# Conditional projection and LoRA, 64 samples on one core: order of SyncE, ScalarE and VectorE in the first two pairs, and two transfers for the adapter stack

## What is computed

```python
# x (64,128,1024) f32; itok_B_1_198, itok_B_0_6 (64,): one index per sample
x = x + einsum('bct,bcd->bdt', x, weights[itok_B_1_198])          # per-sample 128x128 matrix
H = einsum('btd,od->bto', x, W)                                   # W (1024,1024), dense
xa = einsum('btd,brd->btr', x, A[itok_B_0_6])                     # LoRA, rank 16, 8 adapters
x = x + H + einsum('btr,bor->bto', xa, Bm[itok_B_0_6]) * scalings[itok_B_0_6]
```

## Time and profile before

| what | before |
|---|---|
| median of 3 runs | 807.09 us |
| the profiled execution, its own time / its span | 807.68 us / 805.0 us |
| PE busy | 770.3 us (96%) |
| DVE / ACT / POOL busy | 620.4 / 510.4 / 190.7 us (77% / 63% / 24%) |
| chain that ended last | PE 89%, DVE 4%, SPq 3%, DMA 2% |
| first 100 us: PE / DVE / ACT busy | 70.6 / 72.1 / 45.2 us |

### The profile page before, as it was taken

The page is one execution under the profiler, slowest core; times in us unless marked ns, Lnnn a source line. Parts: engine busy times, 40 slices in busy tenths (PEclk is TensorE's granted clock), DMA queues, the critical chain, the costliest instruction groups (busy, mean ns, idle before and its releaser), DMA issues.

```text
span 805.0 us, 16851 instructions
## 1 busy us (share of the span) xinstructions
PE 770.3 (96%) x4456; PEld 728.9 (91%) x4456; DVE 620.4 (77%) x1397; ACT 510.4 (63%) x1186; POOL 190.7 (24%) x428
## 2 busy tenths in 40 slices
PE   6875799999999999999999999999999999999997
PEld 3565699999999999999999999999999999999996
DVE  5695977787877778788777878877787887777864
ACT  3364566667666666776666667666666766666663
POOL 4440211222222122222211222221122222112200
PEclk9888899999999999999999999999999999999998
DMA  8522134344233443432334343233434323343221
GB/s 289 149 93 85 59 119 138 117 143 142 97 106 117 137 133 128 143 105 98 123 129 143 117 143 116 99 124 120 140 117 143 134 93 118 117 137 117 86 87 78
DMA packets 47380, 98.26 MB, mean 122 GB/s; under 512 B 6788, under 2 KB 26244, under 8 KB 47364
## 3 DMA queue, kind: packets, MB, share of 16 engines
q1 hardware_dynamic: 47362, 98.08, 37.0%
q10 hardware_dynamic: 2, 0.00, 0.0%
HBM read 63.45 MB, written 34.60 MB: 122 GB/s over the span
## 4 chain that ended last, share of the span: by engine, by line
PE 89%; DVE 4%; SPq 3%; DMA 2%; issue 1%; ACT 1%; DVEq 0%; ACTq 0%
PE bank L1259 73%; PE o_ps L1295 4%; PE o_ps L1296 4%; PE o_ps L1297 4%; PE bank L1274 3%; SPq L343 1%; DVE x_lo L826 1%; DVE w_lo_raw L1089 1%; DMA out<-o_sb 1%; DMA cond_sb<-cond_idx 1%; DVE w_lo L826 1%; SPq L387 0%; PE bank L1279 0%; SPq L390 0%; ACT x_hi L475 0%
## 5 line engine op out<-in xcount | busy, mean ns | idle before, releaser
L1259 PE MATMUL bank<-w_hi,x_hi 128*128 128x342 f32 (+1 forms) x1240 | 404.5, 326 | 7.7 <-ACT c_sb L475 5.6
L1259 PE MATMUL bank<-w_lo,x_hi 128*128 128x342 f32 (+1 forms) x1240 | 401.4, 324 | 0.0
L1259 PE MATMUL bank<-w_hi,x_lo 128*128 128x342 f32 (+1 forms) x1240 | 400.9, 323 | 0.0
L1259 PEld LDWEIGHTS bank<-w_hi,x_hi 128*128 128x128 f32 x1240 | 234.7, 189 | 17.0 <-ACT c_sb L475 6.9
L1259 PEld LDWEIGHTS bank<-w_lo,x_hi 128*128 128x128 f32 x1240 | 234.4, 189 | 3.3
L1259 PEld LDWEIGHTS bank<-w_hi,x_lo 128*128 128x128 f32 x1240 | 234.7, 189 | 0.0
L826 DVE TENSOR_TENSOR x_lo<-x_raw,x_hi 128x256 fp32r<-128x256 f32 (+1 forms) x279 | 151.0, 550 | 34.2 <-ACT x_hi L475 28.9
L475 ACT ACTIVATE x_hi<-x_raw 128x256 fp32r<-128x256 f32 (+1 forms) x279 | 138.2, 507 | 55.7 <-PE bank L1259 49.8
L292 POOL TENSOR_TENSOR w_lo<-a_ride,w_hi 128x160 fp32r<-128x160 f32 x31 | 16.1, 521 | 541.6 <-ACT w_hi L475 541.6
L475 ACT ACTIVATE c_sb<-bank 128x342 f32<-128x342 f32 x190 | 85.5, 451 | 42.0 <-PE bank L1259 41.3
L475 ACT ACTIVATE o_sb<-o_ps 128x512 f32<-128x512 f32 x124 | 74.2, 598 | 36.2 <-PE o_ps L1297 27.0
(11 more groups left out here) (85 smaller groups left out, 846.5 us busy)
## 6 DMA issues: line engine op xcount, KB each, us to landing
x_raw<-xT SPq DMA_DIRECT2D x64, 512.0 KB, 4.6
out<-o_sb SPq DMA_DIRECT2D x62, 512.0 KB, 2.7
b_stack_raw<-b_split SPq DMA_DIRECT2D x128, 128.0 KB, 2.5
a_now<-lora_a SPq DMA_DIRECT2D x64, 64.0 KB, 3.2
c_raw<-cond_w SPq DMA_DIRECT2D x64, 64.0 KB, 1.8
w_lo_raw<-wB SPq DMA_DIRECT2D x7, 342.0 KB, 6.9
w_hi_raw<-wB SPq DMA_DIRECT2D x5, 342.0 KB, 6.7
out<-x_raw SPq DMA_DIRECT2D x4, 256.0 KB, 2.0
```

The lines of the kernel that those rows point to most:

```text
L1259: last = nc.tensor.matmul(bank[:, lo:hi], x[:, left, c * C:(c + 1) * C], w[:, c, FIRST[o]:FIRST[o] + WIDTH[o]], start=opens and c == 0 and ...
```

## The change

On SP:

- The first transfer is the block b12, then both samples of x. Block b01 and the table of scalings are issued by ACT. Block b21 is issued ahead of the first A, b11 ahead of `lora_b`.
- `b_split` is laid out with the part outermost, so that each part is one transfer of 512 KB. Both are issued ahead of pair 1's A and pair 0's condition matrices, which stood ahead of the sixteen before.
- In pair 1's step both stores of pair 0 stand ahead of pair 3's x, which is issued behind the second.

On PE only the dense blocks change places: b21 ahead of b30, and b31 and b02 ahead of the two `turn` products; b32 ahead of the first `lora`. On ACT, `take_b(0, 0)` moves behind the operands of pair 1, the rides and c, `in_place("9")` behind `copy_c17` to `whole_block("02")`, and `evacuate(0, 1, -1, 0, 1)` ahead of the hi parts of "19", "6" and "12". On DVE some sums and rests change places: "y" comes some twenty instructions earlier, `in_place("18")` and `rest_a001` later or earlier by a few instructions. On POOL the identity is added to b21 before the rides of the first pair. No computation is added or left out.

```diff
-    DENSE = ("b12", "b01", "b30", "b21", "b20", "b10", "b00", "b11", "b31", "b02", "b32", "b22")
+    DENSE = ("b12", "b01", "b21", "b30", "b20", "b10", "b00", "b11", "b31", "b02", "b32", "b22")
...
-        b_split = nc.dram_tensor("b_split", [NAD, 2, R, T], f32, kind="Internal").ap()
+        b_split = nc.dram_tensor("b_split", [2, NAD, R, T], f32, kind="Internal").ap()
...
 # SyncE
+            load_w(sp, "b12")
             load_x(0, 0, 0, 0)
-            load_w("b12")
             load_x(0, 0, 0, 1)
-            load_w("b01")
-            load_w("b30")
-            sp.dma_start(s_tab[:, :], scalings.to_broadcast([P, NAD])).then_inc(s_landed, 16)
+            load_w(sp, "b30")
+            load_w(sp, "b21")
             sp.wait_ge(adapter_landed, 16)
             load_a(0, 0, 0)
...
+            sp.wait_ge(b_hi_ready, 1)
+            sp.dma_start(b_split[0, :, :, :].rearrange("a r o -> (a r) o"), z_hi[0][:, :].bitcast(f32)).then_inc(b_saved, 16)
+            sp.wait_ge(b_lo_ready, 1)
+            sp.dma_start(b_split[1, :, :, :].rearrange("a r o -> (a r) o"), z_lo[0][:, :].bitcast(f32)).then_inc(b_saved, 16)
             sp.wait_ge(first_scaled, 8)
             load_a(0, 0, 1)
             sp.wait_ge(cond_landed, 16)
             load_c(0, 0, 0)
-            sp.wait_ge(b_hi_ready, 1)
-            for a in range(NAD):
-                sp.dma_start(b_split[a, 0, :, :], z_hi[0][a * R:(a + 1) * R, :].bitcast(f32)).then_inc(b_saved, 16)
-            sp.wait_ge(b_lo_ready, 1)
-            for a in range(NAD):
-                sp.dma_start(b_split[a, 1, :, :], z_lo[0][a * R:(a + 1) * R, :].bitcast(f32)).then_inc(b_saved, 16)
-            sp.wait_ge(b_saved, 32 * NAD)
+            sp.wait_ge(b_saved, 32)
             load_b(0, 0, 0)
             step(0, 0)
-            step(0, 1)
+            load_b(0, 1, 0)
+            store(0, 1, -1, 1)
+            load_a(0, 1, 2)
+            store(0, 1, -1, 0)
+            after(sp, lo_ready["u54"], 0, 1, 0)
+            after(sp, lo_ready["a02"], 0, 1, 0)
+            after(sp, lo_ready["u3"], 0, 1, 0)
+            load_x(0, 1, 2, 0)
+            load_x(0, 1, 2, 1)
+            load_c(0, 1, 1)
...
 # ScalarE
             act.dma_start(adapter_sb[:, :], adapter_idx).then_inc(adapter_landed, 16)
+            load_w(act, "b01")
+            act.dma_start(s_tab[:, :], scalings.to_broadcast([P, NAD])).then_inc(s_landed, 16)
...
             in_place("3")
-            hi_a1(0, 1, 1)
-            begin_c02(0, 1)
             evacuate(0, 1, -1, 0, 0)
             turned_xa(0, 1, 0, 1)
+            evacuate(0, 1, -1, 0, 1)
             made(act, "19", "12")
...
             in_place("12")
             hi_u12(0, 1, 1)
-            evacuate(0, 1, -1, 0, 1)
...
 # VectorE
             add("4", slot("lo", "4"), w_block("b11"), w_block("b12"), ALU.subtract)
-            in_place("2")
             made(dve, "i32")
             add("14", slot("lo", "14"), slot("hi", "12"), w_block("b32"), ALU.add)
-            in_place("0")
             in_place("4")
-            dve.wait_ge(w_landed["b31"], 16)
-            add("18", slot("lo", "18"), slot("hi", "12"), w_block("b31"), ALU.add)
+            dve.wait_ge(w_landed["b02"], 16)
+            add("y", slot("lo", "8"), w_block("b12"), w_block("b02"), ALU.subtract)
             in_place("14")
```

More of the change, by code:

```diff
@@ L363, in step @@
                     load_c(i, j, 1)
+            load_w(sp, "b12")
             load_x(0, 0, 0, 0)
-            load_w("b12")
             load_x(0, 0, 0, 1)
-            load_w("b01")
-            load_w("b30")
-            sp.dma_start(s_tab[:, :], scalings.to_broadcast([P, NAD])).then_inc(s_landed, 16)
+            load_w(sp, "b30")
+            load_w(sp, "b21")
             sp.wait_ge(adapter_landed, 16)
             load_a(0, 0, 0)
-            load_w("b21")
-            load_w("b20")
+            load_w(sp, "b20")
+            load_w(sp, "b11")
             sp.dma_start(b_raw[:, :], lora_b.rearrange("a r o -> (a r) o")).then_inc(b_raw_landed, 16)
-            for b in ARRIVAL[5:]:
-                load_w(b)
+            for b in ARRIVAL[6:]:
+                load_w(sp, b)
             sp.dma_start(cond_sb[:, :], cond_idx).then_inc(cond_landed, 16)
@@ L446, in _ @@
             pick_scalings(0, 0, 0)
+            pool.wait_ge(w_landed["b21"], 16)
+            add_identity("b21", 0, 170, 0, 128)
+            add_identity("b21", 1, 298, 0, 44)
             pool.wait_ge(a_landed, 32)
@@ L449, in _ @@
             first_rides("b30")
-            pool.wait_ge(w_landed["b21"], 16)
-            add_identity("b21", 0, 170, 0, 128)
-            add_identity("b21", 1, 298, 0, 44)
             first_rides("b20")
@@ L455, in _ @@
             first_rides("b00")
+            pool.wait_ge(w_landed["b11"], 16)
+            add_identity("b11", 0, 0, 86, 42)
+            add_identity("b11", 1, 42, 0, 128)
             pool.wait_ge(w_landed["b10"], 16)
@@ L711, in _ @@
             hi_of("13", slot("hi", "19"))
+            made(act, "5")
+            in_place("5")
             made(act, "v")
             in_place("15")
-            made(act, "5")
-            in_place("5")
             act.wait_ge(b_raw_landed, 16)
@@ L756, in _ @@
             hi_z12(0, 0, 0)
-            made(act, "9", "f")
-            in_place("9")
             copy_c17(0, 1)
@@ L1145, in _ @@
             first_rest(0)
+            add_identity_c(0, 0)
             sum_u910(0, 0, 1)
-            add_identity_c(0, 0)
             rest_u(0, 0, 1)
             sum_u11(0, 0, 1)
+            rest_c(0, 0)
             rest_u910(0, 0, 1)
-            rest_c(0, 0)
             rest_u11(0, 0, 1)
-            dve.wait_ge(w_landed["b02"], 16)
-            add("y", slot("lo", "8"), w_block("b12"), w_block("b02"), ALU.subtract)
-            in_place("18")
             made(dve, "y")
             add("10", slot("lo", "10"), slot("hi", "6"), slot("lo", "8"), ALU.subtract)
+            in_place("18")
             rest_u67(0, 0, 1)
@@ L1165, in _ @@
             add("11", slot("lo", "11"), slot("lo", "11"), slot("hi", "6"), ALU.add)
+            in_place("7")
+            rest_a001(0, 0, 1)
+            dense_through(dve, "b12", "b31")
+            add("12a", w_block("b31"), w_block("b31"), w_block("b32"), ALU.subtract)
+            rest_z("11", 0, 0, 0)
             rest_z("10", 0, 0, 0)
-            rest_z("11", 0, 0, 0)
-            rest_a001(0, 0, 1)
-            in_place("7")
-            dense_through(dve, "b12", "b31")
+            made(dve, "11a")
             add("9", w_block("b12"), w_block("b12"), w_block("b32"), ALU.subtract)
-            add("12a", w_block("b31"), w_block("b31"), w_block("b32"), ALU.subtract)
+            rest_a03(0, 0, 1)
+            rest_z("12", 0, 0, 0)
             in_place("11")
-            rest_z("12", 0, 0, 0)
-            rest_a03(0, 0, 1)
+            sum_u54(0, 0, 1)
             rest_z("01", 0, 0, 0)
             rest_z("00", 0, 0, 0)
-            sum_u54(0, 0, 1)
             made(dve, "12a")
@@ L1222, in _ @@
             rest_xa0(0, 1)
+            sum_u67(0, 1, 1)
+            rest_u12(0, 1, 1)
             sum_u910(0, 1, 1)
@@ L1402, in _ @@
             dense("b01")
+            made(pe, "i21b")
+            dense("b21")
             pe.wait_ge(first_scaled, 2)
             dense("b30")
-            made(pe, "i21b")
-            dense("b21")
-            pe.wait_ge(first_scaled, 8)
+            pe.wait_ge(first_scaled, 4)
             dense("b20")
+            pe.wait_ge(first_scaled, 6)
             made(pe, "i10")
             dense("b10")
+            pe.wait_ge(first_scaled, 8)
             made(pe, "i00")
@@ L1414, in _ @@
             dense("b11")
+            dense("b31")
+            dense("b02")
             pe.wait_ge(ident_r_ready, 1)
@@ L1417, in _ @@
             turn0(0, 0)
-            dense("b31")
-            dense("b02")
+            made(pe, "i32")
+            dense("b32")
             after(pe, g_ready[1], 0, 0, 0)
@@ L1424, in _ @@
             lora("12", 0, 0, 0)
-            made(pe, "i32")
-            dense("b32")
             made(pe, "i22")
```

77 lines of the change are left out of this document (40 added, 37 removed).

## The result

| what | before | after |
|---|---|---|
| median, same chip (four runs each) | 806.48 us (804.62 to 807.21) | 1013.88 us (1012.5 to 1015.24) |
| ratio, 95% interval | 1 | 1.2569 (1.2546 to 1.2593) |
| profiled execution, its span | 807.68 us, 805.0 us | 1014.96 us, 1012.9 us |

The forecast was 791.0 us, with a range of 786.5 to 798.0. The prediction was wrong by 223 us, in the sign and in the place: the first two pairs did become shorter, and the loop, which it had set aside, lost 7.4 us a pair (from one copy of the adapter stack to the next 30.73 us for 23.35, mean of 24 pairs).

The account below looks back on a forecast made before the run. PE was taken to bound the loop, left alone, and DVE's queue the first pairs, where only waits could go. Gains 8.1 + 6.0 + 1.3 + 1.3 = 16.7 us from 807.7 gave 791.0 us, range 786.5 to 798.0.

Parts of the forecast that it names:

- Stores ahead of pair 3's x: Pair 1's step: earlier store ends ACT's 9.25 us wait for `o_sb` and DVE's wait before "19"; gain 8.1 us (7.0 to 8.1).
- Adapter stack in two transfers and later copy: First pairs: sooner stores and later `take_b` cut DVE's 6.92 us wait to some 0.9; gain 6.0 us (4 to 6.9).
- First transfers and sums: DVE's first stretch: reordered transfers and sums remove part of 2.5 us of waits; gain 1.3 us (0 to 2.5).
- b01 on a second queue: First transfers: b01 on ACT's queue gains nothing; by the skill page's rule the sum would be 1.1 us smaller.
- DVE's waits on PE: Pair 1: DVE's 1.12 us wait before `xa_sum` and some tenths beside it go; gain 1.3 us (0 to 1.3).
- saturated stretch: PE's nearly gapless run from 98.45 us to the end, busy 701 of 707 us; forecast to begin near 82 us.
- PE becomes the bound: Rival, pair 1: DVE lighter than counted, PE's own 24.0 us set the end; 788 us or less, chance 0.08.
- The clock never comes up in pair 1: Slower rival: granted clock 0.50 throughout pair 1, its 24.0 us of PE work becoming 48; 812 us, chance 0.04.

Follow-up runs that it names:

- four blocks: The kernel before with the adapter stack in four blocks of 8 rows a read and 32 small stores: 826.86 us, ratio 1.0239.
- eight-read kernel: The changed kernel with each read of 32 rows made as two reads of 16 rows, layout kept: 788.44 us against 807.76, ratio 0.9765.
- the kernel with x first: The eight-read kernel with SP again issuing pair 3's x ahead of sample 1's store in pair 1's step: 799.22 us, ratio 0.990.
- The kernel with the old layout: The changed kernel with the adapter outermost in DRAM, one-piece reads of 32 rows, and two stores of 8 blocks each: 790.75 us, ratio 0.9783.

## Why the prediction was wrong, point by point

**The step that failed** is in two sentences. "[...] the change leaves the loop alone, so nothing can be won there": `load_b` is called for every pair, and the diff changed its layout. And the price of "the stack's reads, which took 4 us from the first issue at 33.70 to the copy at 37.72": these rows are of a read of 32 rows in one piece, and were used for a read that goes over two pieces. The new layout was costed as a change of the stores alone. As measured the term is 12.9 us for 4.0 us, and it applies to all pairs, not to pair 0 alone. The numbers to see that the loop was at risk stood in the trace: in the loop of before ACT comes to the copy 6.13 us or 6.75 us behind the issue, so a read that takes 4 us is hidden, and one of 12.9 can't be. Put in full on each pair, the difference would be some 6.8 us (12.9 - 6.13), against 7.4 measured. The rival that was missing is "slower, by the stack's read in the loop": as an estimate, 791.0 + 31 x 6.8 = 1002 us, against 1013.9 measured. That this comes out so near is partly luck: in the loop the read takes 14.1 us from issue to copy and not 12.9, and with four blocks the same subtraction would give 2.75 us a pair where 0.47 was measured. The eight-read kernel against after is 225 us, for the form of one access.

All the prediction's rivals lie in pairs 0 to 2. The prediction drew on the page "DMA: Bandwidth & Descriptors" of the Trainium skill, from another section than the one that states the rule, and did not hold the new access against the rule.

**The rest of the prediction** can be held against the eight-read kernel, which does all that the change does but for that read (and issues eight reads where the change has four): 788.4 us (789.0 in the later runs) for a forecast of 791.0.

- *Stores ahead of pair 3's x, 8.1 us (7.0 to 8.1).* Right as to the mechanism, and too small: 8.7 us alone, 10.8 us when undone in the full version, both above the upper end. The term was sized by the wait in the trace of before; once the first wait is gone the second would have been longer, so the two terms don't simply add.
- *Adapter stack in two transfers and later copy, 6.0 us (4 to 6.9).* Right as to the mechanism: the stack is no longer waited for, and both halves of the edit are needed (3.9 and 4.0 us, each undone by itself). No run undoes both. What stands on record is the kernel with x first, which has all but the stores: 7.9 us less than before (807.10 - 799.22), where this term, the next one and that of the waits on PE come to 8.6 us together. (It takes DVE's first block as ended at 33.67; the row gives 33.76, 33.34 + 0.42, which changes nothing.) What the prediction said would stay did not: A was to land at 27.4 and the rides to be ready at 33.3, "of the 6.92 us some 0.9 stay". In the eight-read kernel (POOL's first and last step of the rides):

```profile
25.84 1.86 POOL L268 TENSOR_TENSOR a_ride<-a_now,s_now 128x32 f32<-128x32 f32 x3 [0.44 <-DMA a_now<-lora_a]
...
30.33 0.58 POOL L288 TENSOR_TENSOR a_ride<-a_now,a_ride 128x32 f32<-128x32 f32 x1
```

  A is there at 25.84 and the rides at 30.9, not 33.3, and DVE has no wait between 23.59 and 71.97. SP issues A at 21.53 there, so it took 4.3 us behind the stores against 4.8 without them (19.87 to 24.71), no longer, and what is lost against before is its later issue. The prediction had both stores land at about 27.5 us and A behind them; in after the second had landed at 25.3 (issued at 17.39, 7.9 us to landing). The kernel with the old layout shows that the mechanism exists: with the slower stores A took 6.0 us (22.21 to 28.20), and DVE does wait 1.69 us.
- *First transfers and sums, 1.3 us (0 to 2.5).* Not tested apart. DVE's first sum starts at 7.55 for 9.28, 1.7 us sooner. DVE's waits for POOL's identities in the first stretch were to go; two of the kind still stand there, 0.52 and 1.30 us (for 0.72 and 1.21 before). In the seven profiles with these first transfers the first sum starts at 6.62 to 8.42, so the 1.7 us are one draw of several.
- *b01 on a second queue, nothing taken; by the rule of the Trainium skill, as the prediction worked it out, a loss of 1.1 us.* The loss did not come. The medians show a gain of 0.4 us that is within their scatter, the two spans one of 0.9 us. A gain by sooner issue would agree with what the same section of the Trainium skill, "Issuing engines are not separate DMA queues" in "DMA: Bandwidth & Descriptors", says is saved; no run here shows it beyond doubt.
- *DVE's waits on PE, 1.3 us.* The 1.12 us are gone; not tested apart.
- *The rivals.* "PE becomes the bound", 788 us, is near the number of the eight-read kernel but is not its cause: DVE has no wait over 1 us there, and PE has one of 3.23 us for DVE at 72.45. "The clock never comes up in pair 1" did not come about: in the eight-read kernel the granted clock is 1.00 over 42 to 72 us. Slower had 4 in 100, for that one mechanism, which is not the one that made the kernel slower; the loop's granted clock of 0.89 in after goes with the waits for the stack and is 1.00 in the eight-read kernel (both over 200 to 700 us).

The saturated stretch begins at 80.72 in the eight-read kernel, for a forecast of about 82:

```profile
72.45 0.51 PE L1269 MATMUL bank<-w_hi,x_hi 128*128 128x342 f32 x1 [3.23 <-DVE x_lo L835]
...
80.72 0.42 PE L1269 MATMUL bank<-w_hi,x_hi 128*128 128x342 f32 x1 [0.59 <-ACT c_sb L482]
```

That is 17.7 us sooner than 98.45, and the time is 19.3 us less on the same chip (807.76 - 788.44).

## What to carry to other kernels

When a layout changes, price every transfer that reads or writes it anew, by the shape that its access now has, its outermost dimension first; rows of the old shape say nothing about it. A transfer of the loop that is hidden has a slack that can be read in the trace (here 6.13 us from issue to use); compare its new time with that before setting the loop aside. Past that slack the loop is at risk, but the subtraction isn't the loss: 2.75 us more cost 0.47 us a pair, and 7.6 us more cost 7.4. If a tensor has to lie with few large blocks outermost, move it by several transfers of 16 rows each, or a multiple of 16, rather than by one over the blocks.
